# A decoder layer on one core: a second buffer pair in the third sweep, the first maximum on TensorE, and a longer loop body in the recurrence

## The reference, cut to what matters

```
x = layernorm(x + recurrent_attention(x))   # state = state * sigmoid gate + v k^T, out = state q, per head of 16
x = layernorm(x + cross_attention(x, ctx))  # 16 heads, softmax over 128 keys
x = layernorm(x + ffn(x))
```

```
def act_qdq(x):
    scale = maximum(max(abs(x)) / 32767, 1e-12)
    return clip(round(x / scale), -32768, 32767) * scale
x    = act_qdq(x)
up   = act_qdq(x @ dequant(w_up).T)      # 256 -> 768
gate = act_qdq(x @ dequant(w_gate).T)
sig  = round16(sigmoid(gate))
gate = act_qdq(gate * sig)
o    = act_qdq(gate * up)
out  = o @ dequant(w_down).T             # 768 -> 256
```

## Time and profile before

| | |
|---|---|
| Median of three runs | 2437.17 us (2437.17 to 2446.89) |
| Profiled execution | 2458.95 us, span 2457.2 us, mean granted clock 0.949 |
| TensorE busy | 2201.4 us (90%) |
| VectorE busy | 1668.7 us (68%) |
| ScalarE busy | 1134.1 us (46%) |
| GpSimd busy | 271.6 us (11%) |
| DMA engines (q1) | 17.1% of 16 engines' span, 143.70 MB |
| Instruction queue (q8) | 191 packets, 3.13 MB |

### The profile page before, as it was taken

How to read it: one execution, slowest core, us unless ns; L and a number is a source line. 1 busy time by engine, 2 the same in 40 slices (tenths; PEclk the granted TensorE clock), 3 DMA queues, 4 the chain that set the end, 5 groups by cost and what they waited for, 6 DMA issues and landing times. The chain is left out here.

```text
span 2457.2 us, 74676 instructions
## 1 busy us (share of the span) xinstructions
PE 2201.4 (90%) x30260; PEld 1498.7 (61%) x30260; DVE 1668.7 (68%) x3029; ACT 1134.1 (46%) x1874; POOL 271.6 (11%) x273
## 2 busy tenths in 40 slices
PE   1788888888889895999999999999699999999498
PEld 1466666666666664777777777777444444444387
DVE  5576676666666775666667676766455557987797
ACT  0343333333333342666666666666311117854365
POOL 0100000000000000111111111111000004433221
PEclk9799998998988997999999999999899999999799
DMA  2010000001000001101010101010000003459675
GB/s 85 14 29 21 24 26 20 21 22 27 21 21 23 26 16 48 39 28 38 26 38 26 38 26 38 26 38 13 1 0 0 0 0 138 200 197 360 242 261 173
DMA packets 78436, 146.95 MB, mean 60 GB/s; under 512 B 10131, under 2 KB 63638, under 8 KB 78230
## 3 DMA queue, kind: packets, MB, share of 16 engines
q1 hardware_dynamic: 78230, 143.70, 17.1%
HBM read 82.84 MB, written 60.82 MB: 58 GB/s over the span
## 5 line engine op out<-in xcount | busy, mean ns | idle before, releaser
L1273 PE MATMUL ff_bank<-ff_xq,w_uh 128*128 (+1 forms) x1536 | 457.7, 380 | 6.8 <-ACT ff_whole L1380 6.8
L1273 PE MATMUL ff_bank<-ff_xq,w_ul 128*128 (+1 forms) x768 | 291.3, 379 | 0.0
L1273 PEld LDWEIGHTS ff_bank<-ff_xq,w_uh 128*128 128x128 f16 x1536 | 149.7, 98 | 187.4 <-issue 11.4
L586 ACT ACTIVATE x<-rec_e 128x512 f32<-128x512 f32 x192 | 112.1, 596 | 275.0 <-PE rec_e L475 275.0
L487 PE MATMUL rec_x<-x 32*32 32x64 f32 x8192 | 160.1, 230 | 60.3 <-issue 54.9
L1575 DVE TENSOR_REDUCE ff_top<-ff_bank 128x512 f32 (+1 forms) x192 | 132.8, 692 | 116.5 <-PE ff_bank L1273 116.4
L487 PEld LDWEIGHTS rec_x<-x 32*32 32x32 f32 x8192 | 138.8, 114 | 94.1 <-issue 93.9
L1380 ACT ACTIVATE ff_whole<-ff_bank,ff_coef 128x512 int16<-128x512 f32 x192 | 120.6, 682 | 117.6 <-DVE ff_out L1614 63.4
L686 DVE TENSOR_TENSOR rec_tmp<-rec_x,x 32x256 f32<-32x256 f32 (+1 forms) x192 | 80.8, 421 | 136.6 <-PE rec_x L512 68.5
L650 DVE TENSOR_TENSOR x<-rec_x,rec_until 128x512 f32<-128x512 f32 x256 | 158.7, 682 | 21.7 <-PE rec_x L459 21.7
L1062 DVE TENSOR_REDUCE mneg<-att_s 128x4 f32<-128x512 f32 x256 | 159.0, 684 | 5.5 <-PE att_s L878 4.6
(11 more groups left out here) (229 smaller groups left out, 4385.7 us busy)
## 6 DMA issues: line engine op xcount, KB each, us to landing
gate_scratch<-ff_out SPq DMA_DIRECT2D x28, 768.0 KB, 3.5
ff_in<-gate_scratch SPq DMA_DIRECT2D x28, 768.0 KB, 6.7
product_scratch<-ff_out SPq DMA_DIRECT2D x28, 768.0 KB, 6.0
ff_out<-product_scratch SPq DMA_DIRECT2D x28, 768.0 KB, 5.9
att_x<-in_x SPq DMA_DIRECT2D x32, 256.0 KB, 2.7
att_ctx<-in_ctx SPq DMA_DIRECT2D x32, 256.0 KB, 3.0
att_o<-rec_scratch SPq DMA_DIRECT2D x32, 256.0 KB, 3.7
out<-s_out SPq DMA_DIRECT2D x16, 512.0 KB, 3.3
```

What stands on the lines that cost most here:

```text
L1273: m = T.matmul(bank_[:], weights(wp, kc, a, c), tile[:, xp, kc], start=(i == 0), stop=(i == len(terms) - 1))
```

## The change

In the recurrence TensorE's loop takes six pairs a turn (`TURNS = 6`), five turns for the 30 pairs. What is issued for a pair, and its order, are the same.

The first maximum over the partitions leaves GpSimd. VectorE's column is transposed into one row by TensorE, VectorE reduces the row to one number (`peak`), and TensorE multiplies it by a row of ones, which puts it back into all partitions. VectorE reads it from there for S_X. The three other maxima stay on GpSimd.

In the third sweep a second buffer pair `src2` takes the loads of the odd tiles. It lies over the memory of `xq` that held tiles 0 to 2, so its first loads (tile 3) wait until TensorE has finished these tiles' chunks of sweep 3. The load of tile n+2 now waits for `level` of tile n; in SyncE's order it stands where the load of tile n+1 stood, ahead of the store of the same half of tile n. Each buffer has its own semaphore.

```diff
--- before.py
+++ after.py
@@ -277,6 +277,7 @@
     EXPS = NR + NE - 1
     TAKES = 4 + 2 + 4
     DMAS = 16 * (1 + NC)
+    TURNS = 6
     with ExitStack() as ctx:
         def sb(name, shape, dt=F32):
             return ctx.enter_context(nc.sbuf_tensor(name, shape, dt))
@@ -545,10 +546,10 @@
                 products(0, -1, 0, 1, True, False)
                 pieces(0, 0, 0, True, False, True)
                 products(1, 0, 1, 0, True, True)
-                with pe.Fori(0, (NP - 2) // 2) as j:
-                    for u in range(2):
-                        p, s = 2 * j + 1 + u, (1 + u) % 2
-                        pieces(p, s, j + u, True, True, True)
+                with pe.Fori(0, (NP - 2) // TURNS) as j:
+                    for u in range(TURNS):
+                        p, s = TURNS * j + 1 + u, (1 + u) % 2
+                        pieces(p, s, TURNS // 2 * j + (1 + u) // 2, True, True, True)
                         products(p + 1, p, 1 - s, s, True, True)
                 pieces(NP - 1, 1, (NP - 2) // 2, True, True, False)
                 products(NP, NP - 1, 0, 1, False, True)
@@ -1223,6 +1224,8 @@
         topa = sb("ff_topa", [P, 2])
         sc = sb("ff_scales", [P, 16])
         cf = sb("ff_coef", [P, 2 * FC])
+        peak = sb("ff_peak", [1, 1])
+        ones_row = sb("ff_ones_row", [1, P])
         S_X, R_X, S_U, S_G, R_U, R_G, S_2, R_2, K_2, S_UO, R_O, K_O, K_Y, K_US = range(14)
 
         def one(i):
@@ -1240,6 +1243,8 @@
         ob = sb("ff_out", [P, 2, 2, W])
         with ExitStack() as c3:
             xq = c3.enter_context(nc.sbuf_tensor("ff_xq", [P, NT, 2, KC, TOK], F16))
+        src2 = sb("ff_in2", [P, 2, W])
+        srcs = (src, src2)
         whole4 = sb("s4_whole", [P, 2, 2, W], I16)
         hi = sb("s4_high", [P, 2, 2, W], F16)
         lo = sb("s4_low", [P, 2, 2, W], F16)
@@ -1253,11 +1258,11 @@
         banks = [ctx.enter_context(nc.psum_tensor(f"ff_bank{i}", [P, 512], F32)) for i in range(6)]
         turnb = [ctx.enter_context(nc.psum_tensor(f"ff_turn{i}", [P, 1024], F16)) for i in range(2)]
 
-        q1 = {n: sem("s1_" + n) for n in "whole high low turned kept made maxed".split()}
+        q1 = {n: sem("s1_" + n) for n in "peak row whole high low turned kept made maxed".split()}
         q = {n: sem("ff_" + n) for n in "chain part all ready made rounded sourced fixed prod maxed seen".split()}
         q4 = {n: sem("s4_" + n) for n in "whole high low made summed var rstd shift outs chain".split()}
-        stored, loaded4 = ([[sem(f"ff_{n}{u}{s}") for s in range(2)] for u in range(2)] for n in ("stored", "fetched"))
-        loaded = [sem(f"ff_loaded{s}") for s in range(2)]
+        stored, loaded, loaded4 = ([[sem(f"ff_{n}{u}{s}") for s in range(2)] for u in range(2)]
+                                   for n in ("stored", "loaded", "fetched"))
         stored4 = [sem(f"s4_stored{u}") for u in range(2)]
 
         def part(d, n, s):
@@ -1291,9 +1296,8 @@
                     sp.wait_ge(q["prod"], 4 + 2 * m + s + 1)
                     sp.dma_start(part(d, n, s), ob[:, u, s]).then_inc(stored[u][s], 16)
 
-                def load(m, n, s):
-                    sp.wait_ge(q["fixed"], 2 + 2 * (m - 1) + s + 1)
-                    sp.dma_start(src[:, s], part(g_d, n, s)).then_inc(loaded[s], 16)
+                def load(n, u, s):
+                    sp.dma_start(srcs[u][:, s], part(g_d, n, s)).then_inc(loaded[u][s], 16)
 
                 with sp.Fori(0, NT // 2 - 1) as j:
                     for u in range(2):
@@ -1301,20 +1305,23 @@
                             store(g_d, 2 * j + u, 2 * j + u + 2, u, s)
                 for s in range(2):
                     sp.wait_ge(stored[0][s], 16 * 2)
-                    load(NT, 2, s)
+                    sp.wait_ge(q["fixed"], 2 + 2 * (NT - 1) + s + 1)
+                    load(2, 0, s)
                 for u in range(2):
                     for s in range(2):
                         sp.wait_ge(stored[u][s], 16 * (NT // 2))
                 for u in range(2):
                     for s in range(2):
                         store(u_d, NT + u, u, u, s)
+                sp.wait_ge(q["made"], (NT + 3) * FC)
+                for s in range(2):
+                    load(3, 1, s)
                 with sp.Fori(0, NT // 2 - 2) as j:
                     for u in range(2):
                         for s in range(2):
-                            load(NT + 3 + 2 * j + u, 2 * j + u + 3, s)
+                            sp.wait_ge(q["fixed"], 2 + 2 * (NT + 2 + 2 * j + u) + s + 1)
+                            load(2 * j + u + 4, u, s)
                             store(u_d, NT + 2 + 2 * j + u, 2 * j + u + 2, u, s)
-                for s in range(2):
-                    load(2 * NT - 1, NT - 1, s)
                 for u in range(2):
                     for s in range(2):
                         sp.wait_ge(stored[u][s], 16 * (NT - 1))
@@ -1445,6 +1452,10 @@
                         pe.wait_ge(q1["maxed"], n * 2 * FC + k + 1)
                         chunk_products(T, banks[k % 6], k // FC, k % FC, tile, q1["made"])
 
+                pe.wait_ge(q1["peak"], 1)
+                T.transpose(banks[0][0:1, 0:P], top1[:, 0:1], t["ident"][:]).then_inc(q1["row"], 1)
+                pe.wait_ge(q1["peak"], 2)
+                T.matmul(banks[1][:, 0:1], ones_row[:], peak[:], start=True, stop=True).then_inc(q1["row"], 1)
                 turn(0, 0)
                 with pe.Fori(0, NT // 2 - 1) as j:
                     for u in range(2):
@@ -1496,8 +1507,6 @@
             def _(pool):
                 G = nc.gpsimd
                 pool.wait_ge(q["part"], 1)
-                nc.gpsimd.partition_all_reduce(topa[:, 0:1], top1[:, 0:1], P, RMAX).then_inc(q["all"], 1)
-                pool.wait_ge(q["part"], 2)
                 nc.gpsimd.partition_all_reduce(topa[:], top1[:], P, RMAX).then_inc(q["all"], 1)
 
                 def share(m, s):
@@ -1516,17 +1525,18 @@
                 with pool.Fori(0, NT) as j:
                     for s in range(2):
                         share(j, s)
-                pool.wait_ge(q["part"], 3)
+                pool.wait_ge(q["part"], 2)
                 nc.gpsimd.partition_all_reduce(topa[:, 0:1], top1[:, 0:1], P, RMAX).then_inc(q["all"], 1)
                 pool.wait_ge(q["ready"], 2)
                 for u in range(2):
                     for s in range(2):
                         level(NT + u, s, ob[:, u, s])
-                with pool.Fori(0, NT - 2) as j:
-                    for s in range(2):
-                        pool.wait_ge(loaded[s], 16 * (j + 1))
-                        level(NT + 2 + j, s, src[:, s])
-                pool.wait_ge(q["part"], 4)
+                with pool.Fori(0, NT // 2 - 1) as j:
+                    for u in range(2):
+                        for s in range(2):
+                            pool.wait_ge(loaded[u][s], 16 * (j + 1))
+                            level(NT + 2 + 2 * j + u, s, srcs[u][:, s])
+                pool.wait_ge(q["part"], 3)
                 nc.gpsimd.partition_all_reduce(topa[:, 0:1], top1[:, 0:1], P, RMAX).then_inc(q["all"], 1)
 
                 def power(p, u):
@@ -1550,9 +1560,16 @@
                     dve.sem_inc(q["part"], 1)
                     dve.wait_ge(q["all"], k)
 
+                v.did(V.memset(ones_row[:], 1.0))
                 v.did(V.tensor_reduce(top1[:, 0:1], t["x2_top"][:], AX.X, ALU.max))
-                all_parts(1)
-                v.did(V.tensor_scalar(one(S_X), topa[:, 0:1], 1.0 / QMAX, TINY, ALU.mult, ALU.max))
+                v.wait()
+                dve.sem_inc(q1["peak"], 1)
+                dve.wait_ge(q1["row"], 1)
+                v.did(V.tensor_reduce(peak[:], banks[0][0:1, 0:P], AX.X, ALU.max))
+                v.wait()
+                dve.sem_inc(q1["peak"], 1)
+                dve.wait_ge(q1["row"], 2)
+                v.did(V.tensor_scalar(one(S_X), banks[1][:, 0:1], 1.0 / QMAX, TINY, ALU.mult, ALU.max))
                 v.wait()
                 v.did(V.reciprocal(one(R_X), one(S_X)))
                 v.wait()
...
```

More of the change, by code:

```diff
@@ L1596, in _ @@
                 v.did(V.tensor_reduce(top1[:], topr.rearrange("p (a c) -> p a c", a=2), AX.X, ALU.max))
-                all_parts(2)
+                all_parts(1)
                 v.did(V.tensor_scalar(topa[:], topa[:], one(S_X), 1.0 / QMAX, ALU.mult, ALU.mult))
@@ L1640, in _ @@
                 v.did(V.tensor_reduce(top1[:, 0:1], topg[:], AX.X, ALU.max))
-                all_parts(3)
+                all_parts(2)
                 v.did(V.tensor_scalar(topa[:, 1:2], topa[:, 0:1], one(S_G), 1.0 / (I_MULT * QMAX), ALU.mult, ALU.mult))
@@ L1660, in _ @@
                 v.did(V.tensor_reduce(top1[:, 0:1], topg[:], AX.X, ALU.max))
-                all_parts(4)
+                all_parts(3)
                 v.did(V.tensor_scalar(topa[:, 1:2], topa[:, 0:1], one(K_US), 1.0 / QMAX, ALU.mult, ALU.mult))
```

## The result

| | median us | range, runs |
|---|---|---|
| before, same chip | 2442.03 | 2437.17 to 2455.88, 4 |
| after | 2383.45 | 2382.14 to 2386.31, 4 |

The ratio is 0.9764, 95% interval 0.9735 to 0.9793: faster by 58.6 us. 2403 was forecast, with a range of 2378 to 2426. The direction, the range and the first maximum came out. Two terms were too small: the loop gave some 35 to 40 us instead of 22.5, and the third sweep 15.3 instead of 7.5.

What follows compares the result with a forecast made beforehand. TensorE was taken to bound nearly all of the kernel, transfers the third sweep. Gains of 22.5 + 4.6 + 7.5 = 34.6 us off 2458.95 give 2424.4 profiled, less 21.8 to the runs' median: 2403 us, range 2378 to 2426.

Steps and rivals of the forecast that it cites:

- Part 1: Recurrence, TensorE's loop of six pairs: ten fewer jumps at 2.3 us each, short clock fall included, give 22.5 us.
- I keep their number at 11: Recurrence: the long clock falls of 6.8 us, costing 2.3 us each, stay at 11.
- no long falls any more: Rival for the recurrence: the long clock falls vanish, 25 us more gained, 2378 us; chance 0.13.
- 45 us for the loop: Recurrence, by the skill's instruction fetch rule: straight pairs lose their stalls, so the loop gives 45 us, not 22.5.
- The loop does nothing: Rival for the recurrence: stalls return whole in straight code, only the other two parts gain, 2425 us; chance 0.06.
- slower: Rival for the recurrence: straight pairs stall like head pairs and lose the clock, 36 us more than before, 2473; chance 0.05.
- Part 2: First maximum, moved off GpSimd: 1.4 us instead of 5.94, a gain of 4.6 us.
- the next all-reduce was prepared ahead: After the first sweep: POOL's now first all-reduce is prepared under that sweep; else 5.5 us come back.
- Part 3: Third sweep, loads asked for one tile further ahead: 7.5 us gained, with bounds of none and 16 us.
- full use is 371 GB/s: Third sweep: DMA engines fully busy move 39.3 MB in 106 us, ending at 2304.4, or 9 us earlier.
- at TensorE's pace: Rival for the third sweep: TensorE sets its end, 8.5 us more gained, 2394 us; chance 0.10.
- The wait added on SyncE: Third sweep: tile 3's loads wait for tile 2's matmuls; costed at nothing, or one delay if TensorE were later.

Runs made afterwards that it cites:

- e3: The kernel after with the loop put back to two pairs a turn (TURNS = 2); median 2420.53 us, ratio 0.9891.
- e4: The kernel after with all 30 pairs in one turn, so no jump back on TensorE; median 2361.45 us, ratio 0.9664.
- e9: e3 with 52 more instructions (satisfied waits) ahead of TensorE's loop; median 2414.67 us, ratio 0.9884.
- e10: e3 with 101 more instructions (satisfied waits) ahead of TensorE's loop; median 2411.33 us, ratio 0.9949.
- e1: The kernel before with only its loop of two pairs made six; median 2404.57 us, ratio 0.9834.
- e2: The kernel before with only the third sweep's second buffer pair added; median 2421.85 us, ratio 0.9928.
- e11: e4 with 64 more instructions (satisfied waits) ahead of the loop; median 2355.51 us, ratio 0.9723.
- e6: e4 with the third sweep's load of tile n+1 again sent when tile n is read, both buffers kept; median 2381.38 us, ratio 0.9756.
- e8: e4 with 32 more instructions (satisfied waits) ahead of the loop; median 2361.66 us, ratio 0.9673.
- e12: e4 with 64 more instructions (satisfied waits) in each of the 30 pairs, ahead of their second scores; median 2510.70 us, ratio 1.0373.
- e5: Two pairs a turn as in e3, but the turn begins with products instead of pieces, 13 jumps; median 2373.78 us, ratio 0.9718.

## Why the prediction was right, and where it wasn't

**Part 1, the price of a jump.** "A jump costs 27.2 − 24.9 = 2.3 us with its short fall; ten give 22.5 us." That fewer jumps bring the gain is shown; its size was half of what it is. Ten jumps fewer (e3 to after) shorten the stretch by 49.1 us, 4.9 each, and 14 fewer (e3 to e4) by 60.4, 4.3 each. The working went wrong in what it compared: it took the straight pair of a loop of two, 24.9 us, as what a pair costs without a jump. But that pair lies at one place in the code, and carries stalls of 1.0 to 1.3 us at L487 and up to 1.0 at L512 there every turn; at other places (e4, e9, e10) a straight pair takes from 22.1 us. Of the 49.1 us, 34 are ten pairs that lose their jump (27.56 us on average in e3, 24.15 after), and 16 are the other 15, which come down from 25.23 (the four pairs that keep a jump are 1 us dearer together). Only the first part can be the jump's own. The stretch by its kinds of pair: forecast were 4 x 27.2 + 25 x 24.9 + 11 x 2.3 = 756.6 us; measured are 4 x 27.83 + 25 x 24.15 = 715.2, long falls included. So jump pairs were right within 0.6 us, and straight pairs cost 24.15 instead of 25.9 with their share of long falls.

**The number of long falls.** "I keep their number at 11": 2 were there and 4 in e1. But a loop of two had 7 in e2 and e3, and a body of 30 has 2 to 7 (e11, e6, e4, e8), so the number scatters too much to be laid to the loop alone, and no run removes them. The rival "no long falls any more" (2378) comes nearest in time, and only in part by its own reason: its falls went from 11 to 2, but pairs without stalls came too. The Trainium skill says in "Runtime: NRT & Kernel Launch" (Instruction fetch mechanics) that crossing a block in straight code is mostly hidden: nine pairs of 22.3 to 23.1 us agree, and the others, with stalls of up to 1.9 us in a kernel without any jump (e4), don't. By that rule the prediction had 45 us for the loop, and 35 to 40 came. What gives a pair its long fall stays open.

**"The loop does nothing" and "slower".** Both fell: e1 gains by itself, and the straight pairs of after take 24.15 us on average and 26.4 at worst, where 27.7 on average was needed.

**Part 2, the first maximum.** 1.4 us were forecast and 1.53 measured, so −4.4 for −4.6. The handovers are 0.04 to 0.11 us each. The 1x128 matmul is two instructions, 0.58 us together. That the next all-reduce was prepared ahead is shown by what VectorE waits for it, after the first sweep:

```profile
1975.29 0.23 DVE L1616 TENSOR_SCALAR ff_topa<-ff_topa,ff_scales 128x2 f32<-128x2 f32 x1 [0.61 <-POOL ff_topa L1510]
```

**Part 3, the third sweep.** "At 361 GB/s per 0.97 busy, full use is 371 GB/s." That is the step that failed (361 by 0.97 is 372, which changes nothing). The busy share isn't the part of its rate that an engine gives: at 0.98 it moved 363 GB/s (e6), and at 1.02, with more asked for ahead, 424. What came was the rival "at TensorE's pace", to which 0.10 was given: 16 us as its bound, 15.3 measured. By what the trace shows the end is now set by TensorE and VectorE together, as both have 75.00 of 75.00 us. VectorE's last two products take 4.22 us together, where they took 4.20 at the same place before, so its tail did not shorten. The Trainium skill's 358 GB/s ("DMA: Bandwidth & Descriptors", Where 436 GB/s comes from) is passed by 66 GB/s; the 425 of its "HBM Reference" for a core alone is met. The wait added on SyncE, costed at nothing, cost nothing that shows: the sweep stands at the bound without it.

**The sum.** 22.5 + 4.6 + 7.5 = 34.6 us were forecast. Measured are some 35 to 40 (loop: e1 by its medians, 37 by e3's against after, e1 by its ratio), 4.4 and 15.3, or 55 to 60, which agrees with the 58.6 of the medians. 2383 is inside the range because the range reached down to the rival without long falls, 25 us away; what came instead was 12 to 17 us more from the loop and 8 more from the third sweep. Both terms were too small, and that the sum with them stayed inside is luck.

## What to carry to other kernels

What a loop's jump costs is not the stall behind it alone. A short loop also repeats the stalls of its straight code at the same places every turn, so its straight part is no fair sample of what code costs without a jump: compare with a long straight body. And look where the jump lands, as a loop cut so that it lands in slow matmuls just ahead of a wait gave nearly all that unrolling gave. A DMA share near 1 doesn't say that the transfers are at their rate; if each load waits for the last one's reader, ask for one more ahead before calling the sweep bound by transfers. And take the loss of a periodic pattern from several executions: one profiled execution was 15 us off in the very stretch on which the sum rested.

## What the runs showed of the hardware

- Satisfied waits on TensorE cost some 59 ns an instruction in e12 (64 of them, 3.6 to 3.9 us in each pair), and from nothing visible (32 in e8) to 75 ns (101 in e10) ahead of the loop.
- The clock fell to 1.2 GHz behind each of the 14 jump stalls of 1.8 to 2.4 us before and in e3, all ahead of the short matmuls of L488. In e5, where the jump lands in the 72 ns matmuls of L460 behind a stall of 1.2 to 1.4 us, it stayed at 2.4 GHz, but for the one landing with 1.8 us. Stall and landing change together here, so no run says which of the two keeps the clock up.
- A stall lies at a fixed place in TensorE's instruction stream: 52 instructions more ahead of a loop move it 26 matmuls forward in the loop (e9), and 64 more ahead of straight code move the stalls of every fourth pair to the pair before (e11).
- In the third sweep VectorE's product (1.75 us) and GpSimd's level (1.55 us) hold each other up, and the one that starts first keeps its time. A product that starts 0.5 to 0.7 us behind a level takes 2.4 to 2.7 us (2.66 at 2214.62 us of after), and a level that starts within a product takes 2.43 us (at 2202.78) while the product stays at 1.75.
- 0.98 busy DMA engines moved 363 GB/s, 1.02 busy ones 424 GB/s, with transfers of the same kind; a load's time from issue to landing rose from 6.6 to 10.9 us while the throughput rose by 17%.
